# Inverting softmax denominators as exp(-ln l) on ScalarE with a Newton step on VectorE, in a one-core attention and router layer

## What is computed

```python
q = (x @ wq).reshape(B, T, N_HEADS, HEAD_DIM); k = x @ wk; v = x @ wv
scores = jnp.einsum('bqhd,bkd->bhqk', q, k) * scale          # causal mask
probs = jax.nn.softmax(scores, axis=-1)
out = jnp.einsum('bhqk,bkd->bqhd', probs, v).reshape(B, T, C) @ wo
...
x = x + _layernorm(attn(_layernorm(x)))
x = x + _layernorm(ffn(_layernorm(x)))
```

## Time and profile before

| | |
|---|---|
| median of 3 executions | 3364.37 us (3362.97 to 3367.23) |
| the profiled execution, its own time | 3359.56 us |
| its span | 3357.8 us |
| mean granted TensorE clock | 0.985 of full speed |
| busy: PE, PEld, DVE, ACT, POOL | 95%, 48%, 68%, 48%, 61% |
| DMA | 144.03 MB, mean 43 GB/s |

### The profile page before, as it was taken

The page is one execution under the profiler, slowest core; times in us unless marked ns, Lnnn a source line. Parts: engine busy times, 40 slices in busy tenths (PEclk is TensorE's granted clock), DMA queues, the critical chain, the costliest instruction groups (busy, mean ns, idle before and its releaser), DMA issues.

```text
span 3357.8 us, 45475 instructions
## 1 busy us (share of the span) xinstructions
PE 3199.9 (95%) x15976; PEld 1608.5 (48%) x15976; DVE 2277.2 (68%) x5974; ACT 1605.6 (48%) x3180; POOL 2061.7 (61%) x741
## 2 busy tenths in 40 slices
PE   7899999999999999999999999999999999999997
PEld 3444454455554455544444445444555444554444
DVE  4776777777778677774366667677777776777605
ACT  2334454455555455555333344445555554555552
POOL 1335676776676888777311176677667577778870
PEclk9999999999999999999999999999999999999998
DMA  4422111110101001001211211112010100011000
GB/s 118 113 61 64 51 51 38 50 38 29 51 23 57 23 23 29 29 23 38 64 51 51 80 45 37 43 39 64 23 57 23 39 17 23 23 38 54 8 1 25
DMA packets 133011, 144.03 MB, mean 43 GB/s; under 512 B 28200, under 2 KB 93736, under 8 KB 132784
## 3 DMA queue, kind: packets, MB, share of 16 engines
q1 hardware_dynamic: 132480, 140.72, 14.3%
q10 hardware_dynamic: 304, 0.41, 0.0%
HBM read 72.91 MB, written 16.78 MB: 27 GB/s over the span
## 4 chain that ended last, share of the span: by engine, by line
PE 74%; POOL 10%; DVE 8%; issue 3%; ACT 2%; SPq 1%; DMA 1%; POOLq 0%; ACTq 0%; DVEq 0%
PE ps L1460 14%; PE ps L1488 13%; PE ps L1449 12%; PE ps L1591 11%; PE ps L1414 11%; POOL ds L733 8%; PE ps L1501 3%; DVE mx L1062 2%; PE ps L1550 2%; POOL ds L730 2%; DVE ps L1081 2%; PE ps L1631 2%; PE ps L1645 1%; SPq L625 1%; PE ps L1523 1%
## 5 line engine op out<-in xcount | busy, mean ns | idle before, releaser
L829 ACT ACTIVATE pr<-ps 128x512 f32<-128x512 f32 (+3 forms) x2560 | 1296.4, 533 | 1387.3 <-PE ps L1460 974.8
L733 POOL TENSOR_TENSOR ds<-ds,pr 128x2048 f32<-128x2048 f32 (+1 forms) x360 | 1492.0, 4145 | 140.3 <-ACT pr L829 108.4
L1460 PE MATMUL ps<-qs,ks 98*128 98x512 f32 (+3 forms) x2560 | 1351.5, 535 | 37.8 <-DVE mx L1062 14.3
L1062 DVE TENSOR_REDUCE mx<-ps 128x1 f32<-128x512 f32 x1536 | 1004.2, 681 | 356.9 <-PE ps L1449 349.2
L1449 PE MATMUL ps<-ks,qs 96*128 96x512 f32 (+3 forms) x2560 | 958.8, 386 | 53.1 <-ACT pr L829 23.3
L1460 PEld LDWEIGHTS ps<-qs,ks 98*128 98x128 f32 x2560 | 483.1, 190 | 784.8 <-issue 313.6
L1059 DVE CUSTOM_DVE_ANT_0 ps<-ps,mask_qk 128x128 f32<-128x128 f32 (+3 forms) x1024 | 491.0, 496 | 428.4 <-PE ps L1449 424.9
L1449 PEld LDWEIGHTS ps<-ks,qs 96*128 96x128 f32 x2560 | 487.8, 193 | 313.0 <-ACT pr L829 145.8
L1488 PE MATMUL ps<-pr,vs 128*32 128x512 f32 (+3 forms) x5120 | 612.1, 546 | 0.6 <-POOL pr L740 0.5
L1414 PE MATMUL ps<-xT,wq_sb 128*128 128x512 f32 x1024 | 513.2, 598 | 5.6 <-ACT zs L856 3.1
L1591 PE MATMUL ps<-wo_sb,ao 128*128 128x512 f32 x896 | 453.5, 598 | 0.5 <-DVE q L1051 0.5
(11 more groups left out here) (162 smaller groups left out, 1944.1 us busy)
## 6 DMA issues: line engine op xcount, KB each, us to landing
qs<-q SPq DMA_DIRECT2D x762, 64.0 KB, 2.0
wq_sb<-in_L_attn_wq_dram SPq DMA_DIRECT2D x64, 512.0 KB, 4.0
t<-in_L_attn_x_dram SPq DMA_DIRECT2D x32, 512.0 KB, 6.6
xr<-in_L_attn_x_dram SPq DMA_DIRECT2D x28, 512.0 KB, 4.5
out_dram<-xr SPq DMA_DIRECT2D x28, 512.0 KB, 4.8
wo_sb<-in_L_attn_wo_dram SPq DMA_DIRECT2D x8, 512.0 KB, 5.2
qs<-mT SPq DMA_DIRECT2D x252, 4.0 KB
xT<-in_L_attn_x_dram SPq DMA_DIRECT2D x4, 512.0 KB, 5.8
```

The costliest lines, as they stand in the source:

```text
L733: nc.gpsimd.tensor_tensor(ds[:, :, c0:], ds[:, :, c0:], this, ALU.add).then_inc(added, 1)
L829: nc.scalar.activation(pr[:, k % NS, g, c0:], ps[:, PM + EXP_PLACE[head(n, t, g)] % NPM, c0:], ACT.Exp, scale=SCALE).then_inc(exp_done, 1)
L1062: nc.vector.tensor_reduce(found, seen, AX.X, ALU.max).then_inc(mx_done, 1)
L1460: last = nc.tensor.matmul(ps[:, bank, c0:], ks[0:STK + 2, c:c + P], qs[0:STK + 2, n % NS, g, c0:], start=True, stop=not by_mask)
```

## The change

The reciprocals of all units but the last are replaced. ACT takes the natural logarithm of all of PAUX into `guess` (a view of the first half of hT, 128x512), and in the next slot of its list the exponential of its negative, in place. DVE makes one Newton step: off = -l * guess into PAUX, then (off + 2) * guess into PAUX. The scale follows as before. The four parts and the scale now stand in five slots in a row from `first`, for all units. A table set that is named by hand is loaded ahead of the first exponential. `guess` shares its memory with hT, so three waits are added on ACT: the logarithm waits for the router's products that read hT and for the previous scale, and the copy into hT waits for the scale. The last unit keeps its four chunks of reciprocals and scales.

```diff
--- before.py
+++ after.py
@@ -184,9 +184,10 @@
             if not whole(n - 1):
                 put(2 if by_pe(n - 1) else 6, "PE", "sums", n - 1)
             first, apart = 3 if by_pe(n - 1) else 6 if N == 16 else 7, 2 if by_pe(n - 1) and N > 16 else 1
-            for c in range(TB):
-                put(first + apart * c, "DVE", "recip", n - 1, c)
-            put(first + apart * TB, "DVE", "scale", n - 1)
+            for c in range(2):
+                put(first + c, "ACT", "guess", n - 1, c)
+                put(first + 2 + c, "DVE", "refine", n - 1, c)
+            put(first + 4, "DVE", "scale", n - 1)
         if n + 1 < UN:
             for who in ("PE", "ACT", "SP"):
                 put(rows_slot(n + 1), who, "rows", n + 1)
@@ -246,6 +247,13 @@
     def beside(j):
 
         return slots((j // TB + 1) * NU) > 16
+
+    def turn_unit(j):
+        return (j // TB + 1) * NU + 2 + j % TB
+
+    def lows_before(n):
+
+        return sum(turn_unit(j) < n or turn_unit(j) == n and slots(n) == 16 for j in range(TB * LAST))
 
     def lora(at, t0, j, N):
 
@@ -363,6 +371,7 @@
         t4 = sb("t4", [P, TB, D])
         xT = sb("xT", [P, KT, BLK])
         hT = sb("hT", [P, KT, P])
+        guess = hT[:, 0:KT // 2, :].rearrange("p k c -> p (k c)")
         ks = sb("ks", [P, (NQ + 1) * BLK], F32R)
         vs = sb("vs", [P, (NQ + 1) * TB, HD])
         q1 = sb("q1", [P, BLK], F32R)
@@ -441,6 +450,9 @@
         copied = sem("copied")
         den_ready = sem("den_ready")
         rden_ready = sem("rden_ready")
+        log_done = sem("log_done")
+        guess_ready = sem("guess_ready")
+        off_ready = sem("off_ready")
         ao_ready = sem("ao_ready")
         early_ready = sem("early_ready")
         early_sb = sem("early_sb")
@@ -784,6 +796,7 @@
         @block.scalar
         def _(act):
             act.wait_ge(pool_const, POOL_CONST)
+            nc.scalar.preload_act_table_set("natural_log_exp_and_others")
             nc.scalar.activation(slT[:, 0:HD], ones[:, :], ACT.Exp)
 
             def first_norm(i):
@@ -828,6 +841,22 @@
                 act.wait_ge(st_ready, head(n, t, g) + 1)
                 nc.scalar.activation(pr[:, k % NS, g, c0:], ps[:, PM + EXP_PLACE[head(n, t, g)] % NPM, c0:], ACT.Exp, scale=SCALE).then_inc(exp_done, 1)
 
+            def denominators_guess(n, c):
+
+                if c == 0:
+                    if whole(n):
+                        act.wait_ge(pv_done, UNIT_STEP[n + 1])
+                    else:
+                        act.wait_ge(den_ready, SUMS[n + 1])
+                    if lows_before(n + 1):
+                        act.wait_ge(low_ready, lows_before(n + 1))
+                    if n:
+                        act.wait_ge(ao_ready, n)
+                    nc.scalar.activation(guess, ps[:, PAUX, :], ACT.Ln).then_inc(log_done, 1)
+                else:
+                    act.wait_ge(log_done, n + 1)
+                    nc.scalar.activation(guess, guess, ACT.Exp, scale=-1.0).then_inc(guess_ready, 1)
+
             def values(n):
                 act.wait_ge(pv_done, UNIT_STEP[n + 1])
                 if n >= NAO:
@@ -867,6 +896,8 @@
 
             def lora_turn(j, h):
                 act.wait_ge(ht_ready, 2 * j + h + 1)
+                if h == 0:
+                    act.wait_ge(ao_ready, turn_unit(j) - (slots(turn_unit(j)) == 16))
                 nc.scalar.copy(hT[:, h * KT // 2:(h + 1) * KT // 2, :],
                                ps[:, hturn_bank(j, h), :].rearrange("p (k c) -> p k c", c=P)).then_inc(ht_sb, 1)
 
@@ -906,6 +937,8 @@
                     for stage, *a in at.get(j, []):
                         if stage == "pv":
                             values(*a)
+                        elif stage == "guess":
+                            denominators_guess(*a)
                         elif stage == "q":
                             project(*a)
                         elif stage == "rows":
@@ -1072,16 +1105,24 @@
                     dve.wait_ge(negm_ready, 2 * (n + 1))
                     nc.vector.tensor_reduce(low, negm[:, :, :], AX.X, ALU.add).then_inc(mz_ready, 1)
 
-            def recip(n, c):
-                if whole(n):
-                    dve.wait_ge(pv_done, UNIT_STEP[n + 1])
-                else:
-                    dve.wait_ge(den_ready, SUMS[n + 1])
+            def recip_part(c):
+                dve.wait_ge(den_ready, SUMS[UN])
                 part = ps[:, PAUX, c * P:(c + 1) * P]
                 nc.vector.reciprocal(part, part).then_inc(rden_ready, 1)
 
+            def refine(n, c):
+
+                if c == 0:
+                    dve.wait_ge(guess_ready, n + 1)
+                    nc.vector.scalar_tensor_tensor(out=ps[:, PAUX, :], in0=ps[:, PAUX, :], scalar=-1.0, in1=guess,
+                                                   op0=ALU.mult, op1=ALU.mult).then_inc(off_ready, 1)
+                else:
+                    dve.wait_ge(off_ready, n + 1)
+                    nc.vector.scalar_tensor_tensor(out=ps[:, PAUX, :], in0=ps[:, PAUX, :], scalar=2.0, in1=guess,
+                                                   op0=ALU.add, op1=ALU.mult).then_inc(rden_ready, 1)
+
             def scale(n):
-                dve.wait_ge(rden_ready, TB * (n + 1))
+                dve.wait_ge(rden_ready, n + 1)
                 dve.wait_ge(pv_sb, n + 1)
                 nc.vector.tensor_tensor(ao[:, n % NAO, :], ao[:, n % NAO, :], ps[:, PAUX, :], ALU.mult).then_inc(ao_ready, 1)
 
@@ -1093,7 +1134,7 @@
 
             def scale_part(n, c):
                 here = slice(c * P, (c + 1) * P)
-                dve.wait_ge(rden_ready, TB * n + c + 1)
+                dve.wait_ge(rden_ready, n + c + 1)
                 dve.wait_ge(pv_sb, n + 1)
                 nc.vector.tensor_tensor(ao[:, n % NAO, here], ao[:, n % NAO, here], ps[:, PAUX, here],
                                         ALU.mult).then_inc(ao_ready, 1)
@@ -1233,8 +1274,8 @@
                     for m in items(n, j):
                         maximum(*m)
                     for stage, *a in at.get(j, []):
-                        if stage == "recip":
-                            recip(*a)
+                        if stage == "refine":
+                            refine(*a)
                         elif stage == "scale":
                             scale(*a)
                         elif stage == "q":
@@ -1354,7 +1395,7 @@
                     nc.vector.tensor_tensor(x4[:, i, half], x4[:, i, half], t4[:, i, half], ALU.add).then_inc(t_out_dve, 1)
 
             for c in range(TB):
-                recip(UN - 1, c)
+                recip_part(c)
                 scale_part(UN - 1, c)
             tail_att(0)
             tail_mid(0)
```

## The result

The changed kernel takes **3328.91 us** (median of 4 runs, 3326.88 to 3331.11) against 3365.69 us for the kernel before (4 runs, 3362.97 to 3367.23). The ratio is 0.9892, with a 95% interval of 0.9875 to 0.9909: 1.1% faster. The profiled execution took 3326.88 us, its span is 3325.1 us, and the mean granted clock is 0.986 of full speed; before, the span was 3357.8 us. The spans differ by 32.7 us, the medians by 36.8 us.

A forecast was written before the change was run, and what follows sets the result against it. TensorE, busy 95% of the span, was taken as the bound, so only its waits for VectorE counted. Gains by kind of unit, less 2 us for ScalarE, made 32.5: 3359.6 - 32.5 + 4.8 = 3332 us, range 3304 to 3362.

The forecast's parts named there:

- VectorE's and ScalarE's lengths: Drawn operation lengths times counts: VectorE does 155 us less, 2.46 us per unit; ScalarE 75 us more.
- Units 10 to 12, 42 to 44: Waits on a maximum and the mid norm, plus one short wait behind, come back: 1.5 us each, 9 in all.
- Unit 32: Start of this 16-slot unit after a 64-slot one: waits of 2.4 us and clock loss of 3.4; 4.5 us taken.
- Units 13 and 45: TensorE's waits behind maxima and the clock drop after them: at most 7.2 us, 5 taken each, 10 in all.
- Units 6 to 8, 39, 40: Short TensorE waits, partly masked by q stacks that arrive late: 4.5 us back in all.
- Units 21, 29, 53, 61: These four units were forecast to give back 5.5 us together.
- The other light units: Units 14 to 16, 22 to 24, 30, 31 and twins: GpSimd's additions take back the gain; 1 us in all.
- ScalarE's charge of 2 us: Deduction for places where ScalarE's idle time does not catch up two added 0.6 us passes within about three slots.
- (a): Rival: every TensorE wait of the 60 us ceiling goes, light units too: 3304 us; chance 0.13.
- (b): Rival: VectorE waits for ScalarE's guess, and later ScalarE delays GpSimd's first addition: 3361 us; chance 0.10.
- (c): Rival: logarithm and exponential need separate tables, two loads per unit, 99 us on the path: 3431 us; chance 0.06.
- (d): Rival: full-width VectorE passes cost 1.40 us each, so VectorE saves only 1 us per unit: 3351 us; chance 0.05.

The follow-up runs named there:

- the repeat: The changed kernel, unaltered, run again on one chip beside the version without the Newton step: 3331.24 us, 0.9903 of the kernel before.

## Why the prediction was right

The forecast was 3332 us and a saving of 32.5. The measured time is 3328.91 us; the saving is 36.8 us by these medians, 33.3 in the repeat, and 32.7 between the two profiled spans, to which the points below add up:

- **VectorE's and ScalarE's lengths.** The Newton step's operations took 699 ns where I took 680, and ScalarE's passes 594 and 636 where I took 597. Busy times were forecast at 2122 and 1681 us and came out at 2163 and 1662. The step that failed is the product of count and drawn length: drawn lengths overlap. VectorE got 1.81 us per unit back ((185.3 - 71.2) / 63), not 2.46. The sum did not suffer, since it was built from TensorE's waits.
- **Units 10 to 12, 42 to 44.** Forecast 9 us, measured 12.0 (2.0 each). The mid norm's wait and the wait on the maximum both went; the term for what follows was too small.
- **Unit 32.** Forecast 4.5, measured 3.95. Clock and waits both went, as said.
- **Units 13 and 45.** Forecast 10, measured 6.4. The step that failed: I had the Newton step cost nothing here, and it stands ahead of a maximum that TensorE needs. The two kernels without it gain 5.4 and 5.1 us in them (53.61 and 53.38 to 48.25), which was the forecast. In unit 45 the step also keeps half of the clock's loss: 1.7 us (0.13 x 13.0) where 3.4 had stood.
- **Units 6 to 8, 39, 40.** Forecast 4.5, measured 4.8, but the agreement is luck. In the repeat of the changed kernel (span 3330.7 us, 5.6 longer) the same five units lost 0.6 us against the kernel before. There units 38 and 39 took 60.4 us together instead of 56.6, at a lower clock (first the repeat, then the first trace, each from the start of unit 38 to the end of unit 39):

```profile
1840.60:1901.00 60.40, 55.56 (x289) 28.55 (x289) 40.22 (x101) 18.71 (x44) 0.00 (x0) 0.86 0.17 45
```

```profile
1838.60:1895.20 56.60, 50.83 (x288) 25.45 (x288) 39.80 (x101) 18.36 (x44) 0.00 (x0) 0.97 0.18 48
```

The saving here can be lost to the clock from one execution to the next, with the same instructions. Over all 14 traces the two units take 56.6 to 57.5 us in six (both kernels' own traces among them), 60.3 to 61.9 in seven, and 65.1 with the table loads. A difference of 4 us between two single traces can be this alone.
- **Units 21, 29, 53, 61.** Forecast 5.5, measured 3.5: 1.6 each in units 21 and 53, 0.9 in 61, and 29 lost 0.5.
- **The other light units.** Forecast 1, measured 5.9. Units 24, 30, 31 and 56, behind GpSimd's chain, gave 0.6 together, as said. Units 23, 55 and 62 were wrongly put with them; they gave 1.4, 1.4 and 1.2 us, and units 15 and 47 gave 0.6 each.
- **Heavy units.** Forecast 0; they lost 0.3, all in unit 58, and in the table they keep their length in every experiment.
- **ScalarE's charge of 2 us.** Nothing measurable at one pass of each; the cover is used up, though, for the second cost 22 us.
- **The rest**, which had no term, lost 3.6 us: units 0 to 5 1.8, unit 38 1.6 and what follows the last score matmul 1.0, against 0.8 gained before the first.

So the total agrees partly by luck: three terms were too small by 3, 5 and 0.3 us, and three too large by 4, 2 and 0.5, and the charge of 2 that did not fall due stands against the 4 us that no term had. What is shown is which units gain and why.

**The rivals.** (a) cannot be: with no inversion at all only 45.7 us of its 60 come back. (b) was wrong as to the first pass, since beyond its one long wait VectorE waited for ScalarE 4.0 us in all and GpSimd's chain begins when it did before, but its mechanism exists: with twice the work the chain begins 1.2 us later in units 30 and 56. (c) was priced at 1.6 us per unit, 99 us, and costs 2.3, 143 us, where the table set is not named; the clock had been left out of its price. The Trainium skill ("ScalarE: Activation LUTs", section "What ACT_TABLE_LOAD costs") gives 1.28 us for the load, as measured, and 1.38 us of drain for a switch; the trace shows 0.02 us between the pass and the load behind it, so the drain is not seen here, and the measured 143 us stand where the prediction's estimate from that page's figures, (2 x 2.66 - 1) x 63, gave 272. (d) fell with the groups: 699 ns, not 1.40 us. The change does make the kernel faster by what it says it does: the early place of the work alone does not (1.006 with reciprocals; the new inverse with its scale in the old slot was not run).

## What to carry to other kernels

Price a faster operation unit by unit: where the matmul waits behind that engine the saving is real, where a third engine's chain ends last it is worth nothing until that chain is shortened (GpSimd's here, 44 us by itself). Work moved to an engine with spare time is free only until its gaps are used up, 1.23 us per unit here and not 2.46. Ask of a correction step whether it is needed, and look at what stands behind it on its queue: here a Newton step of two short operations cost a third of what the change brought.

## What was not expected of the hardware

- Small waits cost more through the clock than by themselves. Reciprocals placed close together lengthened TensorE's waits in unit 55 by 0.3 us, and the unit by 3.2; its clock fell from 2.4 to 1.2 GHz for a while, and 0.06 x 56.3 = 3.4 us are missing from full speed. What it did before the drop differs only by short gaps; how the chip decides was not tested.
- An instruction's drawn length is not what it adds to its engine: 0.955 us drawn and 0.735 added for a 128x128 reciprocal out of PSUM, 0.699 and 0.565 for the 128x512 Newton operation, and on ScalarE (1661.8 - 1604.3) / 126 = 0.456 added per pass, with 0.594 and 0.636 drawn (1604.3 us is ScalarE's busy time in the kernel with the passes left out).
- The exponential from SBUF to SBUF took 636 ns where the one from PSUM takes 597; from SBUF to PSUM, in the kernel without the Newton step, it took 614. The Trainium skill ("VectorE: DVE Perf Modes", section "The TRN2 errata — SBUF-src ops pay a fixed extra latency per instruction") says that ScalarE's operations with a source in SBUF carry a longer fixed part; the trace agrees in direction, with 39 ns, though the 614 ns suggest that the destination counts too.
